# One maximum over two neighbouring PSUM banks, with the eight banks shared out four and two

## The reference

```python
x = x + 0.5 * ffn(layernorm(x))     # x and w rounded to a 4-bit float per block of 32, then x_q @ w_q.T + bias
x = x + attn(layernorm(x))          # 16 heads of 8 values, rotary positions
x = x + 0.5 * ffn(layernorm(x))
# attn, per batch and head (S = 512, HD = 8):
scores = q @ k.T / sqrt(HD)         # 512 x 512
attn = softmax(scores)              # over the keys, in float32
out = attn @ v
```

## Time and profile before

| | |
|---|---|
| median of 3 runs | 540.68 us |
| the profiled execution | 540.34 us |
| its span, first to last instruction | 538.5 us |
| TensorE matmul busy | 454.2 us (84%) |
| VectorE (DVE) busy | 439.4 us (82%) |
| ScalarE (ACT) busy | 381.9 us (71%) |
| GpSimd (POOL) busy | 228.4 us (42%) |
| maxima, first and last start | 56.1 and 495.0 us |
| exponent scores, first and last start | 77.0 and 515.6 us |

### The profile page before, as it was taken

One profiled execution on the slowest core, in us unless ns is written; L12 is line 12 of the kernel. 1 busy time (PEld: TensorE's weight loads), 2 busy tenths in 40 slices (PEclk: granted clock), 3 DMA queues, 4 the chain that ended last, 5 costly groups with the idle time before them and its releaser, 6 DMA issues.

```text
span 538.5 us, 8359 instructions
## 1 busy us (share of the span) xinstructions
PE 454.2 (84%) x2564; PEld 152.7 (28%) x2564; DVE 439.4 (82%) x1004; ACT 381.9 (71%) x746; POOL 228.4 (42%) x336
## 2 busy tenths in 40 slices
PE   2150789999989999999999998999899989998941
PEld 1120233332323332333233322323233323222211
DVE  6636799898899979987999889988997798898125
ACT  6557049688877878687868877887777786677730
POOL 8100047424654465535563664456543624113300
PEclk9995589999999999999999999999999999999995
DMA  6012411321122212230122212221222123100000
GB/s 169 15 49 82 142 41 55 91 90 49 40 92 75 80 31 79 73 108 31 54 86 90 70 50 89 91 69 51 85 75 80 30 80 94 56 2 2 22 1 19
DMA packets 27961, 34.86 MB, mean 65 GB/s; under 512 B 6279, under 2 KB 21261, under 8 KB 27917
## 3 DMA queue, kind: packets, MB, share of 16 engines
q1 hardware_dynamic: 26284, 33.94, 20.2%
q10 hardware_dynamic: 1632, 0.39, 0.3%
HBM read 21.34 MB, written 8.39 MB: 55 GB/s over the span
## 4 chain that ended last, share of the span: by engine, by line
PE 52%; DVE 27%; issue 7%; ACT 6%; POOL 4%; DMA 2%; SPq 1%; POOLq 0%; DVEq 0%; ACTq 0%
PE ot L1117 16%; DVE negmax L894 14%; PE sc L1104 14%; PE st L1093 11%; ACT probs L650 2%; PE misc L1042 2%; PE misc L1059 2%; DVE stats_f L763 2%; PE misc L1082 2%; ACT feat_k L540 1%; PE misc L1067 1%; PE misc L1075 1%; DMA feat_k<-parts_k 1%; PE misc L1037 1%; DVE amax_f L786 1%
## 5 line engine op out<-in xcount | busy, mean ns | idle before, releaser
L894 DVE TENSOR_REDUCE negmax<-sc 128x1 f32<-128x512 f32 x512 | 329.7, 682 | 45.8 <-PE sc L1104 45.5
L650 ACT ACTIVATE probs<-st 128x512 f32<-128x512 f32 x512 | 272.8, 599 | 76.7 <-PE st L1093 74.7
L1104 PE MATMUL sc<-feat_k,feat_q 96*128 96x512 bf16 x512 | 186.4, 392 | 14.5 <-DVE negmax L894 11.5
L1093 PE MATMUL st<-feat_q,feat_k 99*128 99x512 bf16 x512 | 155.9, 380 | 8.1 <-ACT probs L650 8.0
L1117 PE MATMUL ot<-probs,vfeat 128*32 128x512 f32 x1024 | 136.2, 604 | 1.1 <-ACT probs L650 1.0
L1104 PEld LDWEIGHTS sc<-feat_k,feat_q 96*128 96x128 bf16 x512 | 49.5, 97 | 163.6 <-DVE negmax L894 100.5
L1093 PEld LDWEIGHTS st<-feat_q,feat_k 99*128 99x128 bf16 x512 | 49.4, 98 | 78.1 <-ACT probs L650 49.2
L1026 PE MATMUL misc<-identb,xq_f 128*128 128x128 bf16 x64 | 6.8, 234 | 36.3 <-DVE xq_f L838 35.8
L418 POOL TENSOR_TENSOR rstd_f<-ve_f,nhalf 128x4 f32<-128x4 f32 x16 | 16.6, 1034 | 46.9 <-DVE nm_f L775 46.9
L459 POOL TENSOR_SCALAR maxparts<-negmax 128x16 bf16<-128x16 f32 x32 | 8.5, 267 | 62.4 <-DVE negmax L894 62.4
L1117 PEld LDWEIGHTS ot<-probs,vfeat 128*32 128x32 f32 x1024 | 20.2, 108 | 37.4 <-ACT probs L650 19.9
(11 more groups left out here) (134 smaller groups left out, 462.6 us busy)
## 6 DMA issues: line engine op xcount, KB each, us to landing
feat_q<-parts_q SPq DMA_DIRECT2D x96, 96.0 KB
feat_k<-parts_k SPq DMA_DIRECT2D x96, 96.0 KB
qkswap<-qkpre SPq DMA_DIRECT2D x32, 128.0 KB, 2.0
parts_q<-qkparts_q SPq DMA_DIRECT2D x24, 128.0 KB, 2.3
parts_k<-qkparts_k SPq DMA_DIRECT2D x24, 128.0 KB, 2.3
xres<-in_L_attn_x_dram SPq DMA_DIRECT2D x8, 256.0 KB, 5.0
out_dram<-xres SPq DMA_DIRECT2D x8, 256.0 KB, 2.5
feat_q<-maxrows ACTq DMA_DIRECT2D x32, 12.0 KB
```

The lines of the kernel that those rows point to most:

```text
L650: nc.scalar.activation(probs[:, s % US, j * S:(j + 1) * S], st[:, bank(2 * s + j), :], ACT.Exp, scale=SCALE).then_inc(exp_done, 1)
L894: nc.vector.tensor_reduce(negmax[:, g, j:j + 1], sc[:, bank(16 * g + j), :], AX.X, ALU.max, negate=True).then_inc(sc_maxed, 1)
L1093: nc.tensor.matmul(st[:, bank(2 * s + j), :], feat["k"][par][0:MROWS, h, kb * P:(kb + 1) * P], feat["q"][par][0:MROWS, h, :], start=True, ...
L1104: nc.tensor.matmul(sc[:, bank(16 * g + j), :], feat["q"][par][0:SROWS, h, t * P:(t + 1) * P], feat["k"][par][0:SROWS, h, :], start=True, s ...
```

## The change

`BANKS` becomes 2; `st` has two banks and `sc` four. `maxima` is called once in a slot, at the place of the first of the two calls, and one TENSOR_REDUCE reads two neighbouring banks (128 x 2 x 512) and writes two columns of `negmax`. It waits for both score matmuls of the slot, and `sc_maxed` counts pairs. TensorE issues both score matmuls of a slot ahead of the two exponent-score matmuls. The first of the pair waits until the pair of maxima two slots back is done; `scoresT` number n waits for exponential n-2, always. The functions `bank` and `back` go. The weight of the set-up passes through bank 3 of `sc`.

```diff
--- before.py
+++ after.py
@@ -49,7 +49,7 @@
 VW = 32
 BLK = 32
 NB = D // BLK
-BANKS = 3
+BANKS = 2
 LEAD = 15
 SCALE = float(1.0 / np.sqrt(HD))
 EPS = 1e-5
@@ -149,7 +149,7 @@
 
 
         st = ctx.enter_context(nc.psum_tensor("st", [P, BANKS, S], F32))
-        sc = ctx.enter_context(nc.psum_tensor("sc", [P, BANKS, S], F32))
+        sc = ctx.enter_context(nc.psum_tensor("sc", [P, 2 * BANKS, S], F32))
         ot = ctx.enter_context(nc.psum_tensor("ot", [P, S], F32))
         misc = ctx.enter_context(nc.psum_tensor("misc", [P, S], F32))
         miscb = misc[:, :].bitcast(BF16)
@@ -216,14 +216,6 @@
 
             return value > 0
 
-        def bank(j):
-
-            return j % BANKS if j < 2 * STEPS - 1 else 1
-
-        def back(j):
-
-            return next(n for n in range(1, 2 * BANKS) if bank((j - n) % (2 * STEPS)) == bank(j))
-
         def hurried(n, b):
 
 
@@ -452,7 +444,7 @@
             def split_max(b, g):
 
                 u = G * b + g
-                pool.wait_ge(sc_maxed, 16 * u + 16)
+                pool.wait_ge(sc_maxed, 8 * u + 8)
                 if after(u):
                     pool.wait_ge(max_turned, u)
                 src = negmax[:, g, :]
@@ -647,7 +639,7 @@
                 act.wait_ge(st_ready, 2 * (STEPS * b + s) + j + 1)
                 if j == 0 and after(4 * (u - 1) + 2 * half + 2):
                     act.wait_ge(pv_done, 4 * (u - 1) + 2 * half + 2)
-                nc.scalar.activation(probs[:, s % US, j * S:(j + 1) * S], st[:, bank(2 * s + j), :], ACT.Exp,
+                nc.scalar.activation(probs[:, s % US, j * S:(j + 1) * S], st[:, j, :], ACT.Exp,
                                      scale=SCALE).then_inc(exp_done, 1)
 
             def slot(b, par):
@@ -741,7 +733,7 @@
             def set_up_parts():
 
                 dve.wait_ge(init_pe, 3)
-                wt = st[:, 2, 0:D]
+                wt = sc[:, 3, 0:D]
                 link(nc.vector.tensor_copy(w3[:, 0, :], wt))
                 link(nc.vector.tensor_tensor(wtmp[:, 0, :], wt, w3[:, 0, :], ALU.subtract))
                 link(nc.vector.tensor_copy(w3[:, 1, :], wtmp[:, 0, :]))
@@ -885,14 +877,14 @@
                     dve.wait_ge(parts_out, 96 * b)
                 nc.vector.tensor_tensor(qkparts[i][:, 2, :], qkrest[i][:, :], qkparts[i][:, 1, :], ALU.subtract).then_inc(qk_low, 1)
 
-            def maxima(b, g, j):
-
-                n = 64 * b + 16 * g + j
-                dve.wait_ge(sc_ready, n + 1)
-                if j == 0 and after(4 * (G * b + g - 3)):
+            def maxima(b, g, i):
+
+                two = 32 * b + 8 * g + i
+                dve.wait_ge(sc_ready, 2 * two + 2)
+                if i == 0 and after(4 * (G * b + g - 3)):
                     dve.wait_ge(max_split, 4 * (G * b + g - 3))
-                nc.vector.tensor_reduce(negmax[:, g, j:j + 1], sc[:, bank(16 * g + j), :], AX.X, ALU.max,
-                                        negate=True).then_inc(sc_maxed, 1)
+                nc.vector.tensor_reduce(negmax[:, g, 2 * i:2 * i + 2], sc[:, 2 * (i % BANKS):2 * (i % BANKS) + 2, :], AX.X,
+                                        ALU.max, negate=True).then_inc(sc_maxed, 1)
 
             def invert_sums(b, g):
 
@@ -928,7 +920,7 @@
                         for nb, _ in turns(b, par, s, n, "mul", first, later=1):
                             add_ffn(n, nb)
                     if has(mb):
-                        maxima(mb, mg, 2 * ms)
+                        maxima(mb, mg, ms)
                     for nb, _, g in pairs(turns_of_unit(b, par, s, OUT["turn"] + 1, -1)):
                         normalise(nb, g)
                         if hurried("f2", nb) and g == G - 1:
@@ -981,8 +973,6 @@
                         for nb, _ in turns(b, par, s, "pj", "low", 2, i=i):
                             if hurried("pj", nb):
                                 low(nb, i)
-                    if has(mb):
-                        maxima(mb, mg, 2 * ms + 1)
                     for n, first in (("f2", -1), ("f1", 2)):
                         for later in (0, 1):
                             for nb, _ in turns(b, par, s, n, "amax", first, later=later):
@@ -1007,7 +997,7 @@
                     ins = nc.tensor.transpose(st[:, i, t * P:(t + 1) * P], qkpre[:, i, t * P:(t + 1) * P], ident[:, :])
             ins.then_inc(init_pe, 1)
             pe.wait_ge(init_vec, WQ_STEP)
-            nc.tensor.transpose(st[:, 2, 0:D], wtmp[:, 1, :], ident[:, :]).then_inc(init_pe, 1)
+            nc.tensor.transpose(sc[:, 3, 0:D], wtmp[:, 1, :], ident[:, :]).then_inc(init_pe, 1)
             pe.wait_ge(init_act, 10)
 
             last = [None]
@@ -1088,20 +1078,20 @@
                 if s % US == 0 and j == 0:
                     pe.wait_ge(max_loaded[g % 2], 16 * (2 * b + g // 2) + 16)
                 n = 2 * (STEPS * b + s) + j
-                if after(n + 1 - back(2 * s + j)):
-                    pe.wait_ge(exp_done, n + 1 - back(2 * s + j))
-                nc.tensor.matmul(st[:, bank(2 * s + j), :], feat["k"][par][0:MROWS, h, kb * P:(kb + 1) * P],
+                if after(n + 1 - BANKS):
+                    pe.wait_ge(exp_done, n + 1 - BANKS)
+                nc.tensor.matmul(st[:, j, :], feat["k"][par][0:MROWS, h, kb * P:(kb + 1) * P],
                                  feat["q"][par][0:MROWS, h, :], start=True, stop=True).then_inc(st_ready, 1)
 
             def scores(b, par, g, j):
 
-                n = 64 * b + 16 * g + j
+                two = 32 * b + 8 * g + j // 2
                 h, t = UH * g + j // T, j % T
                 if j == 0:
                     pe.wait_ge(feat_loaded[g], FEATS * (b + 1))
-                if after(n + 1 - back(16 * g + j)):
-                    pe.wait_ge(sc_maxed, n + 1 - back(16 * g + j))
-                nc.tensor.matmul(sc[:, bank(16 * g + j), :], feat["q"][par][0:SROWS, h, t * P:(t + 1) * P],
+                if j % 2 == 0 and after(two + 1 - BANKS):
+                    pe.wait_ge(sc_maxed, two + 1 - BANKS)
+                nc.tensor.matmul(sc[:, j % (2 * BANKS), :], feat["q"][par][0:SROWS, h, t * P:(t + 1) * P],
                                  feat["k"][par][0:SROWS, h, :], start=True, stop=True).then_inc(sc_ready, 1)
 
             def times_v(b, par, g, kb):
@@ -1129,11 +1119,10 @@
                             times_v(vb, vpar, vg, kb)
                     if has(mb):
                         scores(mb, mpar, mg, 2 * ms)
+                        scores(mb, mpar, mg, 2 * ms + 1)
                     if has(b):
                         scoresT(b, par, s, 0)
                         scoresT(b, par, s, 1)
-                    if has(mb):
-                        scores(mb, mpar, mg, 2 * ms + 1)
                     for nb, _, g in turns_of_unit(b, par, s, MAX["turn"], 1):
                         turn_max(nb, g)
                     for nb, _, g in pairs(turns_of_unit(b, par, s, OUT["turn"], -1)):
```

## The result

The changed kernel takes 568.61 us (median of four runs, 568.17 to 569.34) against 540.63 (540.35 to 541.19): ratio 1.0516, 95% interval 1.0499 to 1.0532, 28.0 us slower. The forecast was 562.2, in a range of 551 to 572. The direction, the place and the size of the main term came out; 6.4 us of the 28 were not forecast, and the time lies just above the 568 at which the prediction's likeliest case ended.

What follows compares the result with a forecast made beforehand. TensorE's written order was taken to set the pace in most slots, VectorE where behind. Terms 12 + 4.5 + 2.1 + 1.8 + 2 - 0.7 = +21.7 us took the profiled 540.34 to 562.0; forecast 562.2, range 551 to 572.

Steps and rivals of the forecast that it cites:

- the prediction's likeliest case: The forecast as it stands, 562.2 us, reaching from 555 to 568; chance 70%.
- The exponent ring: Even slots without placed work: second exponent score waits for the previous slot's second exponential, 0.47 us each, 4.3 a batch.
- The maximum of two banks: On VectorE, a pair takes 1.14 us in place of 1.20: 0.06 less, 15 us over 256 pairs.
- The waits for maxima: TensorE's waits for VectorE's maxima, 2.1 us in a batch, of which 1.9 would be regained.
- the five in the middle: Five middle batches, each +4.3 of exponent waits less 1.9 of waits for maxima, +2.4: +12 us.
- The lead-in: Between 56 and 77 us, maxima without exponent scores: 15 pairs save 0.06 each, less 0.2 for later start: -0.7 us.
- First batch: Six bare slots (+2.8) and two half covered (+0.5), less 1.3 of waits for maxima: +2 us.
- sixth: Batch from 415.2 to 467.8 us: eleven even slots at 0.47 and 0.5 more, less 1.2 of waits: +4.5.
- last batch to the last exponent score: Two parts: last stretch with scores (467.8 to 495.4 us) +2.1, and the end without scores +1.8.
- At the end: Where no scores are left: some 0.36 us for five of the seven even slots, +1.8 us.
- the second: Rival: waits for maxima stay, as VectorE's lumps of 1.14 us hold up short operations; 572 us, chance 10%.
- The third's condition: Rival: a pair of maxima costs 1.36 us, as much as two lone ones; 574 us, chance 6%.

Runs made afterwards that it cites:

- The run with that part alone: Kernel before with two banks for the exponent scores (scoresT n waits for exponential n-2), nothing else changed: 564.16 us, ratio 1.0437.
- the halved exponentials: Exponentials over 256 of 512 columns from the second unit on: in the changed kernel 545.12 us, ratio 1.0080; in the kernel before 540.49, ratio 0.9998.
- the kernel with running banks: Kernel before, three and three banks kept but dealt by running number n % 3 over all batches: 534.81 us, ratio 0.9901.
- the other order in odd slots: Changed kernel with exponent scores issued ahead of the two score matmuls in odd slots: 567.03 us, ratio 1.0496.

## Why the prediction was right, and what it missed

**The exponent ring: right.** The step read the price of a two-back bank from slot 0 of the kernel before (0.47) and applied it to every even slot with nothing placed ahead. Seven slots (2, 6, 8, 16, 20, 22 and 30) show 0.47 each, slots 12 and 14 together 0.47 (0.49 said), slot 10 shows the exponential's wait in place of the maximum's as said, slot 26 0.03. The batch pays 4.3 in these slots, as forecast. The run with that part alone makes it shown, and the halved exponentials (1.34 to 0.91) show that it is their length.

**The maximum of two banks: right in size, wrong in consequence.** One shows 1.22 us as forecast, and in a chain they come 1.13 apart (five in 5.75 us; 1.14 said). I called its gain VectorE's alone. Merging is worth 2.9 us of the whole, since the placed work behind it comes earlier: slots 17, 19 and 23 take 0.23 us less together in a batch.

**The waits for maxima: mis-sized.** Of 2.1 us in a batch I took 1.9 as regained. 1.8 were (slot 10 0.64, slot 11 0.30, slot 17 0.85), but 0.6 came back as new waits in slots 19, 23 and 27: 1.2 net. That is 0.7 in a batch, 3.4 us over the five in the middle. The runs show what did which. With two banks for the exponent scores and nothing else, slots 10, 11 and 17 are already at 1.34, 2.15 and 2.62: 1.7 of the regained time is VectorE catching up during the new waits, which the prediction named last, and not the deeper ring or the merged pair. Four banks of scores bring slot 17 to 2.21, and then all 2.1 are regained. The new order takes back 0.2 (slot 27) and the pair the rest, 0.8 (slots 17, 19, 23). The reason I had not counted: I said nothing is lost by taking both maxima at the first place because the pair starts when the first one did. It ends 0.5 later than the first one did (1.22 us against 0.68), and all placed work of the slot is behind it.

**The lead-in: wrong sign, and in part the clock.** -0.7 said, +0.9 measured (22.44 us in place of 21.54). But the clock rose 1.5 us later in the execution of the changed kernel, and that is in the 0.9. The changed kernel with halved exponentials and the kernel with running banks have the lead-ins of the two kernels, and in both the clock rose at 74.4: 22.79 and 22.48 us, so the change itself adds 0.3. The other 0.6 is the moment of the clock, which is not in my sum. The 1.0 between -0.7 and +0.3 is my miss: I counted VectorE's saving and not that a ring of pairs moves two banks at a time. Here VectorE waits for a whole pair of scores, 0.98 us before the chain of five; that this wait is the loss was not tried by itself.

```profile
73.91 5.75 DVE L886 TENSOR_REDUCE negmax<-sc 128x2 f32<-128x1024 f32 x5 [0.98 <-PE sc L1094]
```

**The rest.** First batch +2.9 (+2 said), sixth +4.9 (+4.5), last batch to the last exponent score +4.6 (+3.9 for its two parts). With +0.9 and 15.4 for the five in the middle (12 said) that is 28.7 against the spans' 28.6; less the 0.6 of the clock it is close to the 28.0 of the medians. At the end the cycle of two slots takes 2.88 us (2.40 before): the whole 0.48 comes through, where I had taken 0.36:

```profile
535.27 0.60 PE L1083 MATMUL st<-feat_q,feat_k 99*128 99x512 bf16 x2
536.35 0.88 PE L1083 MATMUL st<-feat_q,feat_k 99*128 99x512 bf16 x2 [0.47 <-ACT probs L642]
537.16 1.06 PE L1107 MATMUL ot<-probs,vfeat 128*32 128x512 f32 x8
538.15 0.60 PE L1083 MATMUL st<-feat_q,feat_k 99*128 99x512 bf16 x2
```

Of the rivals, the second (waits for maxima stay) had the right sense and the wrong mechanism: those waits go, others come. The third's condition, 1.36 us for a pair, did not occur. No miss cancelled another: every term that was off by more than 0.1 us was off to the same side, so the time came out high in the range. The page of the Trainium skill on grouping (Perfetto Trace Analysis, Optimizing Scalar/DVE Operations) gives 125 ns per instruction on PSUM; in the chains here it is 0.60 x 2 - 1.13 = 0.07 us, and the measurement decides.

The 2 us that the first batch, the sixth and the last miss were not taken apart slot by slot and stay open.

## What to carry to other kernels

Before banks are taken from one ring for another, look for a place in the old trace where the ring is already that short: its wait of 0.47, times nine bare places, gave 4.2 of the 4.3 us in a batch. Price the depth of a ring by the round trip (from the start of the matmul to the end of the reader that the next user waits for: 1.56 us here) against the work between the two starts (1.09), not by the reader's busy share, which was 71%. And when a fixed schedule passes faster or groups two steps into one, follow what is placed behind them. Each of four kernels here that took waits away (the changed one, the halved exponentials, the other order in odd slots, the running banks) got from a third to all of it back as waits for placed work on another engine.

## What was not expected of the hardware

With halved exponentials in the kernel before, TensorE's granted clock fell from 2.4 to 1.2 GHz in the middle of the run, once in each of five batches, in slot 17, right behind a 1.24 us wait. Its eight `times_v` matmuls took 1.87 us in place of 1.06:

```profile
217.42 0.39 PE L1105 MATMUL sc<-feat_k,feat_q 96*128 96x512 bf16 x1 [1.24 <-DVE negmax L895]
217.65 0.39 PE L1027 MATMUL misc<-identb,xq_f 128*128 128x128 bf16 x4
217.97 1.87 PE L1118 MATMUL ot<-probs,vfeat 128*32 128x512 f32 x8
...
217.60:221.20 3.60, 3.60 (x17) 0.80 (x15) 1.98 (x5) 0.94 (x2) 1.97 (x5) 0.57 0.46 135
...
212.00:217.00 5.00, 3.96 (x21) 1.01 (x18) 5.00 (x10) 2.68 (x9) 3.59 (x3) 1.00 0.38 118
```

PE was busy 3.96 of the 5.0 us before. The wait does not explain the fall. The kernel before with the new order waits longer in the same slot (1.38 or more, in each of its batches 1 to 5), was busy less in the same 5 us (3.82), and kept its clock at 2.4 GHz:

```profile
219.47 0.39 PE L1104 MATMUL sc<-feat_k,feat_q 96*128 96x512 bf16 x1 [1.39 <-DVE negmax L894]
...
214.05:219.05 5.00, 3.82 (x20) 0.87 (x17) 5.00 (x10) 3.96 (x9) 3.59 (x3) 1.00 0.36 118
```

What sets the two apart is not shown here and stays open. What is shown is that the fall repeated in every batch from 1 to 5 and took back more than the halved exponentials had gained there. Whether the spread of that kernel's runs (538.99 to 543.98 us) is this clock alone was not tried.
